# A Mamba block and a mixture block in one pipeline: the softplus taken in pairs of blocks, its three sums and both residual sums made by adding transfers, the router's rows in other tiles

## The reference

```python
# block 1 (Mamba), di = 512 channels, N = 16 states
xs, res = split(rmsnorm(x) @ w_in);  xs = silu(conv4(xs));  res = silu(res)
delta, B, C = split(xs @ w_xproj);   delta = softplus(delta @ w_dt + b_dt)      # 512 channels x 512 tokens
h[t] = exp(delta[t] * A) * h[t-1] + (delta[t] * xs[t]) * B[t]                   # for each of 16 states
y = sum_n h[n] * C[n];  out = x + ((y + xs * D) * res) @ w_out
# block 2 (experts), two branches of 8 experts of rank 64
weights = softmax(gelu(q @ w1 + b1) @ w2 + b2 + bias)
out = sum_k weights[k] * ((q @ V_k) * cumsum(k @ W_k)) @ U_k / n
```

## Time and profile before

| | us |
|---|---|
| median of 3 runs | 2472.93 (2469.58 to 2481.07) |
| the profiled execution, its own time | 2463.2 |
| its span | 2461.4 |
| DVE busy in the span | 2187.0 (89%) |
| PE / POOL / ACT busy | 2128.8 / 1854.4 / 1843.2 |
| mean granted TensorE clock | 0.954 |

### The profile page before, as it was taken

The page is one execution under the profiler, slowest core; times in us unless marked ns, Lnnn a source line. Parts: engine busy times, 40 slices in busy tenths (PEclk is TensorE's granted clock), DMA queues, the critical chain, the costliest instruction groups (busy, mean ns, idle before and its releaser), DMA issues.

```text
span 2461.4 us, 35873 instructions
## 1 busy us (share of the span) xinstructions
PE 2128.8 (86%) x9268; PEld 1287.6 (52%) x9268; DVE 2187.0 (89%) x2820; ACT 1843.2 (75%) x3897; POOL 1854.4 (75%) x1324
## 2 busy tenths in 40 slices
PE   5687789898998989899898988989898998988797
PEld 2355455464655546465554646555464655546454
DVE  1889999998999999998999989999999989999931
ACT  6566787868788786978778687887869788785644
POOL 3868697887879788786877868797887879787620
PEclk8797899999999999999999999999999999999999
DMA  6011110111102021110202011020211102011100
GB/s 136 27 39 47 31 44 23 64 32 53 36 20 63 23 66 31 54 35 25 60 23 61 32 56 36 14 69 23 62 31 57 35 16 68 22 54 33 35 1 17
DMA packets 83404, 101.76 MB, mean 41 GB/s; under 512 B 23480, under 2 KB 49872, under 8 KB 83168
## 3 DMA queue, kind: packets, MB, share of 16 engines
q1 hardware_dynamic: 83168, 99.06, 13.7%
HBM read 90.13 MB, written 8.91 MB: 40 GB/s over the span
## 4 chain that ended last, share of the span: by engine, by line
PE 31%; DVE 28%; issue 21%; ACT 10%; POOL 8%; DVEq 1%; ACTq 0%; DMA 0%; POOLq 0%
PE bank L798 16%; DVE h L1348 12%; DVE yT L1364 9%; PE stateT L971 6%; PE bank L950 5%; POOL bx L766 5%; ACT decay L1217 3%; DVE xs L1257 2%; PE bank L936 1%; DVE rows L1283 1%; PE bank L860 1%; ACT rows L1009 1%; DVE st_b L1244 1%; PE bank L952 1%; DVE cumT L1303 1%
## 5 line engine op out<-in xcount | busy, mean ns | idle before, releaser
L766 POOL TENSOR_TENSOR bx<-dx,B_rows 128x1024 f32<-128x1024 f32 x512 | 1204.1, 2364 | 267.7 <-DVE h L1348 265.1
L1348 DVE TENSOR_TENSOR_SCAN h<-decay,bx 128x512 f32<-128x512 f32 x1024 | 1242.5, 1214 | 77.0 <-ACT decay L1217 63.3
L1217 ACT ACTIVATE decay<-delta,decay_rate 128x512 f32<-128x512 f32 x1024 | 705.0, 693 | 305.8 <-DVE h L1348 301.4
L971 PE MATMUL stateT<-ident,h 128*128 128x128 f32 x4096 | 633.2, 286 | 195.6 <-DVE h L1348 104.6
L971 PEld LDWEIGHTS stateT<-ident,h 128*128 128x128 f32 x4096 | 482.2, 145 | 508.5 <-issue 257.1
L1364 DVE SCALAR_TENSOR_TENSOR yT<-stateT,C_tok,yT 128x512 f32<-128x512 f32 x960 | 701.6, 731 | 17.6 <-PE stateT L971 15.8
L798 PE MATMUL bank<-k_to_expert,cumT 128*128 128x512 f32 x512 | 252.9, 618 | 9.4 <-ACT dx L1120 8.8
L798 PE MATMUL bank<-q_to_expert,xnT 128*128 128x512 f32 x512 | 252.9, 619 | 5.2 <-DVE xs L1257 5.2
L798 PE MATMUL bank<-hT,w_in_sb 128*128 128x512 f32 x512 | 244.4, 602 | 4.1 <-DVE xs L1257 1.5
L1183 ACT ACTIVATE cum_sb<-bank,gate 128x64 f32<-128x64 f32 x1024 | 222.0, 324 | 28.0 <-PE bank L798 25.9
L950 PE MATMUL bank<-expert_to_out,prodT 128*128 128x256 f32 x1024 | 238.3, 381 | 0.5 <-ACT cum_sb L1183 0.5
(11 more groups left out here) (155 smaller groups left out, 2596.1 us busy)
## 6 DMA issues: line engine op xcount, KB each, us to landing
B_rows<-B_scratch SPq DMA_DIRECT2D x256, 256.0 KB, 3.3
x_front<-in_L_attn_x SPq DMA_DIRECT2D x16, 512.0 KB, 6.0
x_back<-in_L_attn_x SPq DMA_DIRECT2D x16, 512.0 KB, 6.6
out<-x_back SPq DMA_DIRECT2D x16, 512.0 KB, 3.4
w_in_sb<-in_L_attn_w_in SPq DMA_DIRECT2D x1, 1024.0 KB, 5.8
cum_sb<-in_L_ffn_V_fwd SPq DMA_DIRECT2D x2, 256.0 KB
prod<-in_L_ffn_W_inv_exp SPq DMA_DIRECT2D x2, 256.0 KB
xnT<-in_L_ffn_W_fwd SPq DMA_DIRECT2D x2, 256.0 KB
```

Source lines behind the costliest of these rows:

```text
L766: pool.tensor_tensor(bx[use % BX_RING][:, :, :], dx[q.parity][:, 2 * half:2 * half + 2, :], row, ALU.mult).then_inc(s_bx.step(f"{n},{half} ...
L971: last = pe.transpose(stateT[j % 2][:, c * P:(c + 1) * P], h[n % 2][:, c, j * P:(j + 1) * P], ident[:, :])
L1217: act.activation(decay[c % 2][:, :], delta[q.parity][:, c, :], ACT.Exp, scale=decay_rate[:, c, n:n + 1]).then_inc(s_exp.step(f"{n},{c}"), 1)
L1348: dve.tensor_tensor_scan(h[n % 2][:, c, :], decay[c % 2][:, :], bx[(2 * n + c // 2) % BX_RING][:, c % 2, :], 0.0, ALU.mult, ALU.add).then_ ...
```

## The change

1. The softplus runs on pairs of blocks: exp, 1 + e, ln and the rounded rest are activations of 128x1024 in place of two of 128x512 (`ex`, `ln` have two entries in the timetable, not four).
2. Its three sums are transfers with an add, from SBUF to SBUF, 128x1024 f32 (512 KB) each, issued by POOL: w adds into e's pair, w2 into `dx`, d1 into `delta`. Each waits until the one before it has landed (`w_added`, `r_added`, `d_added`). Before, w and w2 were 4 instructions each on POOL and d1 was 4 on DVE.
3. The two residual sums are such transfers too (x1: 512 KB, waited for by `st1`; x: 512 KB, waited for by SP's store).
4. The router's hidden rows leave `scratch` and stand in one tile with `rows` and `x_front`; SP therefore loads the next `x_front` only after the step lg of the batch two before.
5. Every beat of the timetable is set anew.

```diff
-    ("F", "ex", "act"): (91, 97, 109, 119),
-    ("F", "w", "pool"): (101, 103, 119, 126),
+    ("F", "ex", "act"): (82, 107),
+    ("F", "w", "pool"): (93, 117),
...
+        rows_and_front = sb("rows_and_front", P, 2 * TB, D)
+        rows, x_front = rows_and_front[:, 0:TB, :], rows_and_front[:, TB:2 * TB, :]
+        hidden = rows_and_front[:, :, :].rearrange("p (a b) d -> p a (b d)", b=2)
...
             def load_x_front(batch, k, use):
+                if batch.shift(-2).exists:
+                    sp.wait_ge(b_pe.sem, b_pe.done(batch.shift(-2), "lg"))
...
-            def w_task(b, c, use):
-                e, v = scratch[:, c % 2, :], scratch[:, 2 + c % 2, :]
-                pool.wait_ge(f_act.sem, f_act.done(b, f"u{c}"))
-                pool.tensor_tensor(v, e, v, ALU.subtract).then_inc(f_pool.step(f"w{c}"), 1)
-            def w2_task(b, c, use):
-                v = scratch[:, 2 + c % 2, :]
-                pool.wait_ge(f_pool.sem, f_pool.done(b, f"w{c}"))
-                pool.tensor_tensor(v, v, dx[b.parity][:, c, :], ALU.add).then_inc(f_pool.step(f"w2{c}"), 1)
+            def w_task(b, p, use):
+                pool.wait_ge(f_act.sem, f_act.done(b, f"u{p}"))
+                pool.dma_start(pair(scratch, 0), pair(scratch, 1), accum_op=ALU.add).then_inc(w_added[p], 16)
+            def w2_task(b, p, use):
+                pool.wait_ge(w_added[p], b.count(16, 16))
+                pool.dma_start(pair(dx[b.parity], p), pair(scratch, 0), accum_op=ALU.add).then_inc(r_added[p], 16)
+            def d1_task(b, p, use):
+                pool.wait_ge(r_added[p], b.count(16, 16))
+                pool.dma_start(pair(delta[b.parity], p), pair(dx[b.parity], p), accum_op=ALU.add).then_inc(d_added[p], 16)
             def dx_task(b, c, use):
-                pool.wait_ge(f_dve.sem, f_dve.done(b, f"d1{c}"))
+                pool.wait_ge(d_added[c // 2], b.count(16, 16))
...
             def x1_task(b, k, use):
                 pool.wait_ge(b_act.sem, b_act.done(b, "t3"))
-                pool.tensor_tensor(x_back[b.parity][:, :, :], x_back[b.parity][:, :, :], rows[:, :, :], ALU.add).then_inc(b_pool.step("x1"), 1)
+                pool.dma_start(x_back[b.parity][:, :, :], rows[:, :, :], accum_op=ALU.add).then_inc(back_added, 16)
...
             def dt_task(b, c, use):
-                if c >= 2:
-                    act.wait_ge(f_pool.sem, f_pool.done(b, f"w{c - 2}"))
+                if c == 2:
+                    act.wait_ge(r_added[0], b.count(16, 16))
...
-            def d1_task(b, c, use):
-                dve.wait_ge(f_pool.sem, f_pool.done(b, f"w2{c}"))
-                dve.wait_ge(f_act.sem, f_act.done(b, f"ln{c}"))
-                dve.tensor_tensor(delta[b.parity][:, c, :], delta[b.parity][:, c, :], scratch[:, 2 + c % 2, :], ALU.add).then_inc(f_dve.step(f"d1{c}"), 1)
```

More of the change, by code:

```diff
@@ L130 @@
[L130 to L157, removed]
@@ L170 @@
+    ("L", "store", "sp"): (476,),
 }
@@ L334, in program @@
         l_dve = Steps(sem("l_dve"), steps_of("dve", "L", {"pr": ["pr{}"]}))
-        l_pool = Steps(sem("l_pool"), ["ve", "rs", "ng", "nm", "x0", "x1"])
+        l_pool = Steps(sem("l_pool"), ["ve", "rs", "ng", "nm"])
+        w_added, r_added, d_added = ([sem(f"{n}_added{i}") for i in range(2)] for n in ("w", "r", "d"))
         xf_in = sem("xf_in")
+        back_added, out_added = sem("back_added"), sem("out_added")
         xb_in = [sem(f"xb_in{i}") for i in range(2)]
@@ L1131, in ln_task, with ex_task @@
-            def ln_task(b, c, use):
-                e, v = scratch[:, c % 2, :], scratch[:, 2 + c % 2, :]
-                act.activation(delta[b.parity][:, c, :], e, ACT.Ln, bias=one[:, 0:1]).then_inc(f_act.step(f"ln{c}"), 1)
-                act.wait_ge(f_act.sem, f_act.done(b, f"v{c}"))
-                act.activation(v, v, ACT.Identity, bias=minus_one[:, 0:1]).then_inc(f_act.step(f"u{c}"), 1)
+            def ex_task(b, p, use):
+                e, v = flat(scratch[:, 0:2, :]), flat(scratch[:, 2:4, :])
+                act.wait_ge(f_act.sem, f_act.done(b, f"ab{2 * p + 1}"))
+                act.activation(e, e, ACT.Exp, scale=-1.0).then_inc(f_act.step(f"ex{p}"), 1)
+                act.wait_ge(f_act.sem, f_act.done(b, f"ex{p}"))
+                if p == 1:
+                    act.wait_ge(w_added[0], b.count(16, 16))
+                act.activation(v, e, ACT.Identity, bias=one[:, 0:1]).then_inc(f_act.step(f"v{p}"), 1)
@@ L1138, in xnT_task, with ln_task @@
+            def ln_task(b, p, use):
+                e, v = flat(scratch[:, 0:2, :]), flat(scratch[:, 2:4, :])
+                act.activation(flat(delta[b.parity][:, 2 * p:2 * p + 2, :]), e, ACT.Ln, bias=one[:, 0:1]).then_inc(f_act.step(f"ln{p}"), 1)
+                act.wait_ge(f_act.sem, f_act.done(b, f"v{p}"))
+                act.activation(v, v, ACT.Identity, scale=-1.0, bias=one[:, 0:1]).then_inc(f_act.step(f"u{p}"), 1)
             def xnT_task(b, t, use):
@@ L1154, in gelu_task @@
                 act.preload_act_table_set("gelu_and_others")
-                act.activation(scratch[:, :, :], scratch[:, :, :], ACT.Gelu).then_inc(b_act.step("gelu"), 1)
+                act.activation(hidden[:, :, :], hidden[:, :, :], ACT.Gelu).then_inc(b_act.step("gelu"), 1)
                 act.preload_act_table_set(EXP_SET)
```

183 lines of the change are left out of this document (102 added, 81 removed), and 8 rows, old and new, of the table TIMETABLE.

## The result

The changed kernel takes 2540.52 us (median of 4 runs, 2533.53 to 2546.17), the kernel before 2472.33 on the same chip: ratio 1.0268, interval 1.0231 to 1.0306. It is slower by 2.7%, where 1.2% faster was forecast, and above the range given. The profiled execution of the changed kernel takes 2537.87 us with a span of 2535.8, so the spans differ by 74.4 us.

The account below looks back on a forecast made before the run. DVE, 95% busy, was taken to bound the middle, and a chain of single steps the ends. Against 2463.2 us, -35 - 21 + 25 = -31 gave 2432, times 1.004 a median of 2442 us; range 2405 to 2520.

Parts of the forecast that it names:

- step 5: The two ends: first scans +18.5 us, tail +3.0 and +3.8 us, as nothing hides the transfers; together +25 us.
- R: Time of one adding transfer from POOL's issue to its landing; forecast 5.4 us for 512 KB.
- step 4: Adding transfers: estimates R from rows of loads and stores, 1.6 + 2 x 1.9 = 5.4 us.
- The 3.2 us for a plain copy: Adding transfers: the Trainium skill's price, about 2.0 us plus bytes over 436 GB/s, for 512 KB.
- step 6: Middle periods: other work hides the transfers, costing nothing; softplus cover holds to R = 6.2, x1's has 0.4 us to spare.
- step 2: Middle periods: DVE's wait for PE's router logits goes as dt products move earlier; 1.5 us a period, 21 us.
- step 1: DVE's d1 additions go, four a batch, 2.4 us of DVE's time over 15 periods; 35 us won.
- the freed time isn't taken: Middle: PE, busy 127.9 of 143.2 us a period, could become the bound; 2480 us, chance 0.12.

Follow-up runs that it names:

- e9: Changed kernel with every adding transfer replaced by a POOL instruction at the transfer's own place, d1 too; 2509 us.
- e2: Changed kernel with the three softplus sums as instructions (d1 on DVE), residual sums still transfers; 7 us apart from all five as instructions (2518).
- e8: Kernel before with PE's dt products of blocks 0 and 1 at beats 86 and 87, not 82 and 83; logits' wait 23.8 us, total time not given.
- e14: Kernel before with d1 left out on every engine; -16 us by the ratio (interval -10 to -22).
- e11: Kernel before with only d1 moved, from DVE to POOL right behind w2; +7 us by the ratio.
- e16: Kernel before with half the contraction left out in PE's expert products, and d1 left out besides; leaving out d1 is worth 36 us against e15.
- e5: Changed kernel with L's rstd on POOL at beat 452 and DVE's two cumsums at 322 and 323; slot 7's idle time stays 3.5 us, total not given.
- e13: Changed kernel with silu at beat 65, proj at 71, dt at 75 and 76; slots 8 and 9 lost 7.8 and 7.5 us, total not given.
- e15: Kernel before with half the contraction left out in PE's expert products cum and xv; 11 us slower than before.
- e4: Kernel before with its 12 looped periods written out; 1.0% less than before by the ratio, span 37.7 us shorter.

## Why the prediction was wrong

**The two ends** (step 5, +25 us): +27.1 measured, in part by luck. The start is right: the scan of block 2 begins at 90.06 (91.4 forecast), 17.2 us later, of which 9.6 are the transfers' and 7.6 stay in e9 (its start is 84.0, before 76.4), with the pairs and d1 on POOL. The tail grew by 13.1 us, not 6.8: the transfers' part is 5.9 to 6.5 (e9, e2), but 7.2 us stay in e9 without them. The first period, for which no step stood, was 3.2 us shorter and hid half of that.

**R** (step 4, 5.4 us): 4.6 to 5.3, so 0.1 to 0.8 less. The 3.2 us for a plain copy, which the prediction names beside it, is below every one of them (the shortest took 4.5). **Cover in the middle** (step 6, 0 us): the transfers cost 13.5 us more there than POOL instructions do, a small error. POOL waits for landings (2.3 us ahead of dx in the period shown below); how much of that reaches DVE these runs don't say.

```profile
1391.12 2.51 POOL L707 TENSOR_TENSOR dx<-delta,xs 128x512 f32<-128x512 f32 x2 [2.31 <-DMA delta<-dx]
```

**The logits' wait** (step 2, -21): the wait fell by 18.5 us, as forecast, but the dt products' place wasn't the reason (e8): the wait follows the clock in lg. The size was right by luck, and DVE waits for PE elsewhere now.

**d1 off DVE** (step 1, -35): the step that failed first. The busy time went, the time didn't: worth 16 us in the kernel before by e14, 7 us of loss when POOL does it (e11), 36 with half of the expert products out (e16). The rule behind it, that in the middle work taken off DVE counts at its whole length since DVE is busy 95%, is wrong: in slot 13 PE is as full as DVE, and e14 got 0.6 us in slot 12 and lost 0.7 in slot 13, with PE at a lower clock there. How much of that is PE's fullness and how much its clock stays open.

**The new beats as a whole** (no step): the larger part of the miss. I looked up the few entries that spoke for the forecast (dt, gelu, lb, st1) and costed the rest of the timetable at nothing, without naming what covered what. The middle of e9, which has them, the pairs, the tiles and d1 on POOL, is 34 us longer than before. One entry, xv1 five beats later, is worth 18 us in the changed kernel. Slots 7 and 8 lost 1.5 us a period, of which silu's cover is 0.7; that putting it back would win it wasn't shown, since both attempts (e5, e13) opened larger gaps behind it. The largest loss, 2.9 us a period in slots 0 and 1 (2.2 of it waits for PE's stateT and banks), no run was aimed at, and its cause stays open. The rival "the freed time isn't taken" had the mechanism, PE as the bound, but stopped at 2480: it saw in PE only a limit on the gain, and not that new beats could add gaps.

## What to carry to other kernels

An engine's share in a long stretch hides slots: before pricing work taken off the busiest engine, look at the windows of the very slots it stands in, and count only what the second engine's full slots leave. In a hand-timed order no entry is free: when a row moves by five beats, ask which gap it opens on its own engine and who is queued behind the next wait; a single entry was worth 18 us here, and two put back alone cost 87. Before blaming an engine for a wait, look up when it wrote the very tile that is read, and look at the granted clock beside a wait for PE. And write out the hot loop early, since here that alone beat every other version.

## What was not expected of the hardware

Less work made TensorE slower: without half of the expert products the granted clock over the span was 0.897 (before: 0.954), slot 13 ran at 0.50, and the kernel took 0.44% longer, with each product of its slow stretches taking twice as long. In e15 and in the changed kernel such stretches follow gaps in PE's work, but gaps alone don't tell: before, gaps of 1.72, 1.12 and 1.20 us in slot 12 were followed by a slot 13 at 1.00. What lets the clock fall these runs don't show.

A DVE addition with both inputs in SBUF took 3.19 us behind POOL's bx and 1.23 without. Transfers that add took 4.6 to 5.3 us for 512 KB (medians by tile), and none of the 96 of the softplus more than 6.8, with DVE busy beside them 91% of the middle.

Writing out the loop shortened the span by 37.7 us in the kernel before and 36.9 in the changed one; of PE's waits the trace of before puts only 10.6 us down to issue. So most of what a jump back costs stands under other names. One of them can be named: in e4's middle DVE waits 8.3 us for the logits in place of 23.9, and in ten periods, where the clock is 1.00, not at all.
